# Two additions of product halves written as one-operand sums, in the last layer of a four-layer graph network

## The reference, cut to what matters

```python
h = jax.nn.relu(edge_feat @ W1 + b1)
w = (h @ W2 + b2).reshape(e, 4, MUL, MUL)          # MUL = 8: 256 weights for each edge
w_000, w_011, w_101, w_110 = (w[:, 0], w[:, 1], w[:, 2], w[:, 3])
s_e, v_e = s[src], v[src]                           # 8 scalars, 8 vectors of 3 of the source node
m0 = ALPHA * (einsum('ei,eio->eo', s_e * sh0[:, None], w_000)
              + C110 * einsum('eim,em,eio->eo', v_e, sh1, w_110))
m1 = ALPHA * (einsum('ei,em,eio->eom', s_e, sh1, w_011)
              + einsum('eim,eio->eom', v_e * sh0[:, None, None], w_101))
out0 = segment_sum(m0, dst); out1 = segment_sum(m1.reshape(e, 24), dst)
```

## Time and profile before

| | before |
|---|---|
| median of 3 runs | 6759.45 us (6754.65 to 6770.3) |
| the profiled execution, its own time | 6756.3 us |
| its span, first to last instruction | 6754.5 us |
| busy share of the span: PE, DVE, ACT, POOL | 78%, 58%, 43%, 61% |
| mean granted TensorE clock | 0.689 of full speed |
| instructions | 124961 |

### The profile page before, as it was taken

One profiled execution on the slowest core, in us unless ns is written; L12 is line 12 of the kernel. 1 busy time (PEld: TensorE's weight loads), 2 busy tenths in 40 slices (PEclk: granted clock), 3 DMA queues, 4 the chain that ended last, 5 costly groups with the idle time before them and its releaser, 6 DMA issues.

```text
span 6754.5 us, 124961 instructions
## 1 busy us (share of the span) xinstructions
PE 5258.6 (78%) x43024; PEld 4062.3 (60%) x43025; DVE 3937.8 (58%) x7842; ACT 2910.4 (43%) x7150; POOL 4128.8 (61%) x4168
## 2 busy tenths in 40 slices
PE   6777777776777766755556769999999999999997
PEld 3367767776666666721112436777776777777766
DVE  4366666666666666620001027777777777777777
ACT  4444434343443433410000016666666666666665
POOL 0677777777777777710000027777777777777774
PEclk8555555555555555567667977787878777777877
DMA  8744444444444444489999961111111111111111
GB/s 270 265 164 175 172 164 164 173 173 164 164 164 172 175 164 164 180 325 386 387 387 378 387 211 28 27 27 27 27 27 27 27 27 28 28 28 27 27 27 20
DMA packets 512177, 1005.50 MB, mean 149 GB/s; under 512 B 180257, under 2 KB 247906, under 8 KB 478306
## 3 DMA queue, kind: packets, MB, share of 16 engines
q1 hardware_dynamic: 289890, 453.14, 19.4%
q10 hardware_dynamic: 88800, 475.02, 17.8%
q0 software_dynamic: 133120, 71.57, 6.5%
HBM read 521.51 MB, written 476.05 MB: 148 GB/s over the span
## 4 chain that ended last, share of the span: by engine, by line
POOL 59%; issue 19%; DMA 15%; PE 4%; ACT 1%; DVE 1%; POOLq 0%; SPq 0%; ACTq 0%; DVEq 0%
POOL gathered L506 59%; DMA arena<-adj 9%; DMA arena<-counts 4%; PE psum L710 2%; PE psum L884 1%; PE psum L888 1%; DMA rel_table<-arena 1%; ACT table_out L542 0%; PE psum L736 0%; PE psum L767 0%; DMA rel_table<-table_out 0%; ACT arena L542 0%; DMA arena<-in_L_gnn_weight 0%; PE psum L949 0%; DMA arena<-arena 0%
## 5 line engine op out<-in xcount | busy, mean ns | idle before, releaser
L506 POOL DMA_INDIRECT gathered<-x_rows,idx x2048 | 2065.5, 1009 | 1725.8 <-issue 1725.8
L506 POOL DMA_INDIRECT gathered<-rel_table,idx x2048 | 1998.0, 976 | 632.1 <-issue 632.1
L591 ACT COPY arena<-psum 128x512 f32<-128x512 f32 x1024 | 604.2, 590 | 1580.6 <-PE psum L817 1551.1
L949 PE MATMUL psum<-w,arena 65*128 65x256 f32 x4096 | 1231.8, 454 | 2.3 <-DVE arena L1392 2.3
L949 PEld LDWEIGHTS psum<-w,arena 65*128 65x128 f32 x4096 | 914.9, 231 | 301.3 <-issue 130.0
L817 PE MATMUL psum<-arena 64*128 64x64 bf16 (+1 forms) x12288 | 534.8, 254 | 536.7 <-DVE arena L1188 497.0
L767 PE MATMUL psum<-gathered,arena 128*128 128x32 f32 x4096 | 826.2, 380 | 150.1 <-DMA gathered<-rel_table,idx 148.1
L767 PEld LDWEIGHTS psum<-gathered,arena 128*128 128x128 f32 x4096 | 815.2, 309 | 165.1 <-issue 151.7
L767 PE MATMUL psum<-arena 128*128 128x184 f32 x4096 | 895.8, 379 | 3.4 <-DVE acc L1217 3.4
L767 PEld LDWEIGHTS psum<-arena 128*128 128x128 f32 x4096 | 861.1, 237 | 40.6 <-issue 3.9
L817 PEld LDWEIGHTS psum<-arena 64*128 64x128 bf16 x12288 | 494.1, 120 | 577.4 <-issue 561.2
(11 more groups left out here) (173 smaller groups left out, 5339.8 us busy)
## 6 DMA issues: line engine op xcount, KB each, us to landing
adj<-arena ACTq DMA_DIRECT2D x128, 2048.0 KB
arena<-adj SPq DMA_DIRECT2D x128, 2048.0 KB, 19.8
counts<-arena ACTq DMA_DIRECT2D x128, 1024.0 KB
arena<-counts SPq DMA_DIRECT2D x64, 2048.0 KB, 20.0
rel_table<-table_out ACTq DMA_DIRECT2D x16, 2048.0 KB, 7.5
rel_table<-arena ACTq DMA_DIRECT2D x16, 2048.0 KB, 7.6
gathered<-rel_table,idx POOLq DMA_INDIRECT x2048
arena<-in_edge_attr SPq DMA_DIRECT2D x128, 256.0 KB
```

The costliest lines, as they stand in the source:

```text
L506: pool.indirect_dma_start(gathered[:, s, j, :], None, rows[l], bass.IndirectOffsetOnAxis(ap=idx[:, s, j:j + 1], axis=0),).then_inc(rows_in ...
L591: act.copy(w_to, made[:, 0]).then_inc(w_out, 1)
L949: mm = pe.matmul(pair[g % 2][:, WN * q:WN * q + WN], hidden[:, s % 2, q, P * g:P * g + P], w2[:, :], start=True, stop=True)
```

## The change

The two additions of halves, each a tensor_tensor with two operands in SBUF, become tensor_reduce instructions with one operand: the same product tile is read whole, in an order in which the two elements to be added stand next to each other (`k`, of two), and they are summed over that axis. The output is the same tile, of the same size. Waits, signals and their places stay as they are, and so does everything on the other engines.

```diff
                     dve.wait_ge(a_ready, group + 1)
-                    dve.tensor_tensor(split(to[:, :, 0:MA], MUL), prod_a[:, :, :, 0:MUL], prod_a[:, :, :, MUL:],
-                                      ALU.add).then_inc(half_a, 1)
+                    dve.tensor_reduce(split(to[:, :, 0:MA], MUL),
+                                      prod_a[:, :, :, :].rearrange("p j o (k i) -> p j o i k", k=2), AX.X, ALU.add
+                                      ).then_inc(half_a, 1)
                     dve.wait_ge(pair_free, group + 3)
                     half = prod_v[:, :, :, :, :].rearrange("p j m o i -> p j (m o) i")
-                    dve.tensor_tensor(split(to[:, :, MQ:MSG], 4), half[:, :, :, 0:4], half[:, :, :, 4:8], ALU.add
-                                      ).then_inc(half_v, 1)
+                    dve.tensor_reduce(split(to[:, :, MQ:MSG], 4), half.rearrange("p j n (k i) -> p j n i k", k=2),
+                                      AX.X, ALU.add).then_inc(half_v, 1)
```

## The result

| | before | after |
|---|---|---|
| median | 6759.97 us of 4 runs (6754.65 to 6770.3) | 6644.38 us of 4 runs (6641.89 to 6648.3) |
| ratio, 95% interval | | 0.9829 (0.9816 to 0.9841) |
| span of the profiled execution | 6754.5 us | 6641.2 us |
| busy share: PE, DVE, ACT, POOL | 78%, 58%, 43%, 61% | 78%, 64%, 44%, 60% |
| mean granted TensorE clock | 0.689 | 0.701 |

The kernel is 115.6 us faster.

What follows compares the result with a forecast made beforehand. POOL's gathers were taken as the bound, 21.01 us a chunk. With DVE and PE then pacing at 20.6, 128 chunks gain 52 us and the tail loses 4: 6759 - 48 = 6711, said as 6710 us, range 6650 to 6790.

Steps and rivals of the forecast that it cites:

- What bounds the kernel, and what holds a gather: POOL's gathers set the pace at 21.01 us a chunk; DVE instructions with two SBUF operands hold gathers, 132 us in all.
- Held until that run was over: A 1.89 us gather was held from about 0.12 us after its start until the run L1401, L1405, L1408 ended.
- POOL's term, -103 us: On POOL's gathers: 29 of 132 us of holding stay, so 20.2 us a chunk in place of 21.0.
- The price of the sums, +0.67 us a group: On DVE: L1401 goes from 415 to 681 ns, L1405 from 553 to 952; +2.66 us a chunk.
- That gives 19.95 + 0.65 = 20.6 us a chunk; DVE with PE, no longer POOL, sets the pace: DVE's work plus its leftover waits for PE exceed POOL's 20.2 us a chunk; chance 0.50.
- Its first term, DVE's work of 19.95 us a chunk: DVE's work without waits, 17.3 us from a chunk with hardly a wait, plus 2.66 for the longer sums.
- Its second term, "I take 0.65 us a chunk, a sixth of the 3.6, as left over": DVE's waits for PE's weights, 3.6 us a chunk, shrink to 0.65; ends 0 and 1.2.
- POOL keeps the pace: Rival: all of DVE's waits are covered, POOL bounds at 20.2 us a chunk, 6660 us; chance 0.14.
- The tail, +4 us: After the last gather nothing is hidden: six groups at 0.67 us more on DVE add 4 us.
- The longer loop (slower): Rival: DVE with PE, between L1392 and L949, becomes slower than 21.01 us a chunk; 6781 or 6838 us; chance 0.22.
- That tensor_tensors don't hold POOL: Rival: two-operand instructions are not what holds gathers, POOL stays at 21.01 us a chunk, 6763 us; chance 0.12.

Runs made afterwards that it cites:

- the filler: Kernel before, both additions with two operands, plus in every group a one-operand tensor_reduce of 512 elements, result unused; 6822.88 us, ratio 1.0094.

## Why the prediction was right and wrong

- **What bounds the kernel, and what holds a gather:** right. The chain named POOL; single rows named the run of two-operand instructions and the point of 0.12 us. Experiments on order, on one addition at a time and on cadence all agree.
- **"Held until that run was over":** right for most. In the kernel before 334 gathers were held by the run of three for more than 0.02 us, 269 of them until the end of L1408 and 65 only until the end of L1401 or L1405; each release lies within 0.01 us of such an end. What decides between them was not settled.
- **POOL's term, -103 us:** the mechanism was right, the size small by a sixth. It measured -121.7. I left 29 us of holding; 10.5 are left. The sum took the whole length of an instruction as time in which a gather is held until its end. The traces show less: a lone L1401 of 0.41 us held none whose point came in its first 0.13 us, and 0.29 us was the longest hold; L1370 of 0.56 us held by 0.38 us at most. With the longest hold in the place of the length, an estimate made afterwards, random phase gives 11, 25, 99 and 192 us for the changed kernel, the one with only `prod_v` reduced, the changed order and the filler; measured are 10.5, 24.2, 91.2 and 198.4. Only the kernel before lies far off it, 132 for 196.
- **The price of the sums, +0.67 us a group:** right, 679 and 957 ns.
- **"That gives 19.95 + 0.65 = 20.6 us a chunk; DVE with PE, no longer POOL, sets the pace":** this is the step that failed. Both terms were too big. They measured 19.5 and 0.4 us, and POOL kept the pace at 20.06, the rival that was given 0.14 at 6660 us.
- **Its first term, DVE's work of 19.95 us a chunk**, decided it. With 19.5 in its place even the 0.65 gives 20.15, below the 20.2 forecast for POOL; with 0.4 in the place of 0.65 alone it is 20.35, and DVE stays the bound. The price of the sums was right, so the error lay in the 17.3 us of work before. The chunk that I called one with hardly a wait had more waiting than its one row shows: in it L1385 started 0.50 and 0.30 us after L1408 where 0.17 us is the distance with nothing to wait for. PE's groups start 3.60 us apart there, and DVE's own work on a group is 3.45. The filler kernel shows the work bare. Its shortest chunk is

```profile
4585.83 0.56 DVE L1372 TENSOR_TENSOR cprod<-gathered,sh 128x384 f32<-128x384 f32 x1 [0.55 <-issue]
...
4605.09 0.56 DVE L1372 TENSOR_TENSOR cprod<-gathered,sh 128x384 f32<-128x384 f32 x1 [0.53 <-issue]
```

  19.26 us, less four fillers of 0.59 us 16.9; and 16.9 + 2.66 is the 19.5 of the changed kernel's shortest chunk.
- **Its second term, "I take 0.65 us a chunk, a sixth of the 3.6, as left over":** 51/128 = 0.4 us is left, and it costs nothing, since 19.5 + 0.4 is still below POOL's 20.06. The wait is what the period leaves beside DVE's work: it fell from 458 us to 258 with the filler, 185 with only `prod_v` reduced, 51 in the changed kernel and 16 with DVE as the bound. DVE stood ready too early, as the prediction said itself, and once it was later it stopped waiting. I should have believed that sentence and not kept a share for safety.
- **The range** ended at 6650 since POOL's gain was taken as 103; at the 132 that the same part gives as its upper end the case "POOL keeps the pace" reaches 6631. The end of a term was worked out and then not carried into the range. The terms as measured give the result: 6759 - 121.7 for the stretch, + 4.7 for the tail, + 3.7 for the later first gather is 6646 us.
- **The tail, +4 us:** right, 68.5 for 63.8 us.
- **The longer loop (slower):** it exists, but its point was not reached. With 1.33 us of DVE work more a chunk DVE does set the pace.
- **That tensor_tensors don't hold POOL:** refuted, as the prediction expected with 0.88. The Trainium skill, "SBUF — State Buffer", "Who interferes with whom", infers that a tensor_tensor leaves descriptor generation alone; the runs show up to 0.96 us of holding for one gather.

## What to carry to other kernels

Where an engine issues indirect DMAs at its limit, look for issues that take longer than the shortest, and ask what DVE was doing a fixed time after their start: runs of instructions with two SBUF operands held them here. By the estimate at random phase their cost grows with the square of a run's length, so cutting a run by reordering, which brought 35 us here, is worth trying before paying for it in DVE time. Extra work on an engine with waits is free until its own work reaches the period of the bound; the number to compare is its work without any wait, small hidden ones too. Take it from the sum of the distances start to start with nothing to wait for, not from the shortest chunk: that one still held 0.7 us of waits here (17.55 for 16.9). When waits exist because an engine is early, they vanish when it is later.

## What the runs showed that was not expected

- How even POOL is: in five kernels its idle time between two of the 2048 gathers is never under 0.303 nor over 0.317 us.
- L1217 has two SBUF tensors of 32 elements besides its column, and is 0.25 us long, yet held none: in the changed kernel 47 gathers had their point in it, and the longest was 0.021 us over; in the kernel with the order changed it was 0.035 us, of 67. L1408 in the kernel with only `prod_v` reduced, 96 elements behind a tensor_reduce, held none of 33 by more than 0.005 us; in the changed kernel, also behind a tensor_reduce, L1409 held 92 gathers by 0.045 us on average. Why these differ was not settled.
- A gather held in L1401 mostly waits for L1405 and L1408 too, 42 times in the kernel before; but 24 times it was let go at the end of L1401. The one here ends at 4683.42 us, 0.82 us after L1401; held until the end of L1408 it would have ended at 4684.06:

```profile
4682.19 0.41 DVE L1401 TENSOR_TENSOR arena<-arena 128x256 f32<-128x256 f32 x1
4682.21 1.21 POOL L506 DMA_INDIRECT gathered<-x_rows,idx  x1 [0.30 <-issue]
4682.52 0.55 DVE L1405 TENSOR_TENSOR arena<-arena 128x384 f32<-128x384 f32 x1
4682.99 0.25 DVE L1408 TENSOR_TENSOR arena<-q_sum,sh 128x96 f32<-128x96 f32 x1
```
